# DLRM tower on one core: tiles written out, and masks made from ids in 7 gapped rows of 37

## The reference, cut to what matters

```python
e = jnp.stack([tbl_0[ids[:, 0]], ..., tbl_26[ids[:, 26]]], axis=1)   # [2048, 27, 128], fp32
interactions = jnp.einsum('bfd,bgd->bfg', e, e).reshape(B, 27 * 27)
z = jnp.concatenate([bottom_mlp_out, interactions[:, TRIL_IDX]], axis=1)   # 128 + 351 columns
h = jnp.concatenate([z, bottom_mlp_out], axis=1)                           # 607 columns
h = jnp.maximum(h @ W_top1 + b_top1, 0.0)    # 512
h = jnp.maximum(h @ W_top2 + b_top2, 0.0)    # 256
y = h @ W_top3                               # [2048, 1]
```

## Time and profile before

| | us |
|---|---|
| median of 3 runs | 727.62 |
| lowest and highest | 723.96, 727.86 |
| span of the profiled execution, first to last instruction | 506.4 |
| median less that span | 221.2 |

### The profile page before, as it was taken

One profiled execution on the slowest core, in us unless ns is written; L12 is line 12 of the kernel. 1 busy time (PEld: TensorE's weight loads), 2 busy tenths in 40 slices (PEclk: granted clock), 3 DMA queues, 4 the chain that ended last, 5 costly groups with the idle time before them and its releaser, 6 DMA issues.

```text
span 506.4 us, 7367 instructions
## 1 busy us (share of the span) xinstructions
PE 388.1 (77%) x2708; PEld 353.3 (70%) x2708; DVE 260.2 (51%) x641; ACT 165.4 (33%) x263; POOL 345.1 (68%) x324
## 2 busy tenths in 40 slices
PE   0440878899899589996899589987999689985726
PEld 0440767888788578885788478876888678875516
DVE  0754654945593429742693439551884359330310
ACT  1312252234414323243404433343314341340421
POOL 5877377877787778777877778777877778750000
PEclk9975897999999989997999889997999799997967
DMA  6467212232223221422142221422142222220000
GB/s 154 154 188 218 86 46 64 56 123 63 65 71 107 64 68 45 128 62 62 41 131 63 63 55 46 129 60 70 39 135 62 67 52 52 54 59 10 0 15 1
DMA packets 24792, 38.34 MB, mean 76 GB/s; under 512 B 9436, under 2 KB 17125, under 8 KB 24776
## 3 DMA queue, kind: packets, MB, share of 16 engines
q0 software_dynamic: 10240, 20.99, 15.9%
q1 hardware_dynamic: 14536, 17.12, 11.6%
HBM read 35.00 MB, written 0.01 MB: 69 GB/s over the span
## 4 chain that ended last, share of the span: by engine, by line
POOL 47%; issue 16%; PE 16%; DMA 9%; DVE 6%; ACT 3%; SPq 3%; POOLq 0%; DVEq 0%
POOL rows L203 47%; DMA pairs<-in_tbl 5%; PE gram_bank L531 4%; PE mlp_bank L545 4%; DVE mask L422 3%; PE mlp_bank L556 3%; PE col_bank L506 3%; SPq L229 2%; DMA rowid<-in_row_of_chunk 2%; PE col_bank L492 2%; DVE pairs L455 2%; ACT pairs L334 1%; DMA rows<-in_tbl,idx 1%; ACT eT L322 1%; DMA x<-pairs 1%
## 5 line engine op out<-in xcount | busy, mean ns | idle before, releaser
L203 POOL DMA_INDIRECT rows<-in_tbl,idx x320 | 344.9, 1078 | 106.6 <-issue 96.6
L492 PE MATMUL col_bank<-mask,parts 125*128 125x256 f32 x896 | 121.4, 295 | 46.1 <-DVE mask L422 44.4
L492 PEld LDWEIGHTS col_bank<-mask,parts 125*128 125x128 f32 x896 | 115.0, 201 | 53.7 <-issue 45.1
L531 PE MATMUL gram_bank<-eT 128*122 128x104 f32 x1024 | 119.1, 274 | 19.4 <-DVE pairs L455 8.1
L531 PEld LDWEIGHTS gram_bank<-eT 128*122 128x122 f32 x1024 | 114.8, 189 | 24.9 <-issue 13.3
L422 DVE TENSOR_SCALAR mask<-hot_f,rowid 125x256 fp32r<-125x256 f16 x448 | 131.4, 362 | 0.1
L446 DVE COPY eT<-col_bank 128x512 f32<-128x512 f32 x56 | 59.2, 1057 | 110.6 <-PE col_bank L506 108.7
L322 ACT ACTIVATE eT<-col_bank 128x512 f32<-128x512 f32 (+1 forms) x56 | 55.2, 986 | 168.7 <-PE col_bank L492 101.1
L455 DVE COPY pairs<-gram_bank 26x208 f32<-26x208 f32 x128 | 65.2, 510 | 86.1 <-PE gram_bank L531 84.8
L334 ACT ACTIVATE pairs<-gram_bank 26x208 f32<-26x208 f32 x128 | 67.1, 524 | 85.0 <-PE gram_bank L531 83.9
L545 PE MATMUL mlp_bank<-x,w 126*128 126x256 f32 (+5 forms) x288 | 64.2, 379 | 15.8 <-DMA x<-pairs 15.8
(11 more groups left out here) (10 smaller groups left out, 10.6 us busy)
## 6 DMA issues: line engine op xcount, KB each, us to landing
hot_i<-in_hot_ids SPq DMA_DIRECT2D x8, 896.0 KB
rows<-in_tbl,idx POOLq DMA_INDIRECT x320
pairs<-in_tbl SPq DMA_DIRECT2D x7, 500.0 KB
x<-in_bottom SPq DMA_DIRECT2D x8, 128.0 KB, 2.5
x<-pairs SPq DMA_DIRECT2D x16, 39.0 KB
x<-pairs SPq DMA_DIRECT2D x16, 34.5 KB
w<-in_w SPq DMA_DIRECT2D x1, 512.0 KB
w<-in_w_pairs SPq DMA_DIRECT2D x2, 252.0 KB
```

Of the source, the lines that this page charges most:

```text
L203: pool.indirect_dma_start(out=rows[:, h, n * D:(n + 1) * D], out_offset=None, in_=tables[f], in_offset=bass.IndirectOffsetOnAxis(ap=idx[:, ...
L492: last = nc.tensor.matmul(col_bank[b][:, i * TILE:(i + 1) * TILE], parts[0:ROWS, k, part, c * D:(c + 1) * D], mask[0:ROWS, k % MASKS, c, : ...
L531: last = nc.tensor.matmul(gram_bank[s % 2][0:GRAM_ROWS, q, 0:PACK * (F - 1)], eT[:, a:a + PACK, :].rearrange("p s f -> p (s f)")[:, 0:GRAM ...
```

## The change

All hardware loops are replaced by Python loops, so that every tile is written out. The ids of a table are stored as 7 rows of 37 with one unused element behind each row (a pitch of 38), in `hot_i` and `hot_f`. A mask instruction reads the 7 x 37 ids and writes one run of 259 elements; the matmul takes the first 256. The number of mask instructions, their place in DVE's order and all waits stay. The id DMA and ACT's conversion go over 266 instead of 256 elements a table.

```diff
+ID_ROWS, ID_WIDE = 7, 37
+ID_PITCH = ID_WIDE + 1
+MASK_WIDE = ID_ROWS * ID_WIDE
+MASK_PITCH = MASK_WIDE + 1
+assert MASK_WIDE >= TILE and ID_ROWS % 2 == 1 and MASK_WIDE % 2 == 1
...
-        mask = sb("mask", [128, MASKS, CHUNKS, TILE], f32r)
-        hot_i = sb("hot_i", [128, ONE_HOT, TILE], i32)
-        hot_f = sb("hot_f", [128, ONE_HOT, TILE], fp16)
+        mask = sb("mask", [128, MASKS, CHUNKS, MASK_PITCH], f32r)
+        hot_i = sb("hot_i", [128, ONE_HOT, ID_ROWS * ID_PITCH], i32)
+        hot_f = sb("hot_f", [128, ONE_HOT, ID_ROWS * ID_PITCH], fp16)
...
-            with pool.Fori(0, TILES // 2) as u:
+            for u in range(TILES // 2):
...
-            with sp.Fori(0, (TILES - 4) // 2) as u:
+            for u in range((TILES - 4) // 2):
...
-            with act.Fori(2, TILES - 1) as t:
+            for t in range(2, TILES - 1):
...
+                ids = hot_f[0:ROWS, k, :].rearrange("p (r i) -> p r i", r=ID_ROWS)[:, :, 0:ID_WIDE]
                 for c in chunks:
-                    last = nc.vector.tensor_scalar(mask[0:ROWS, k % MASKS, c, :], hot_f[0:ROWS, k, :],
+                    last = nc.vector.tensor_scalar(mask[0:ROWS, k % MASKS, c, 0:MASK_WIDE], ids,
                                                    rowid[0:ROWS, c:c + 1], None, ALU.is_equal)
...
-            with dve.Fori(1, TILES - 1) as t:
+            for t in range(1, TILES - 1):
...
-                                    mask[0:ROWS, k % MASKS, c, :], start=(c == 0 and part == 0),
+                                    mask[0:ROWS, k % MASKS, c, 0:TILE], start=(c == 0 and part == 0),
...
-            with pe.Fori(2, TILES - 1) as t:
+            for t in range(2, TILES - 1):
```

More of the change, by code:

```diff
@@ L214, in load_hot_ids @@
             def load_hot_ids(t):
-                src = hot_ids_d[bass.ds(t, 1)].rearrange("a k s -> a (k s)").broadcast_to([128, ONE_HOT * TILE])
+                src = hot_ids_d[bass.ds(t, 1)].rearrange("a k s -> a (k s)").broadcast_to([128, ONE_HOT * ID_ROWS * ID_PITCH])
                 sp.dma_start(hot_i[:, :, :].rearrange("p k s -> p (k s)"), src).then_inc(hot_ids_loaded, 16)
@@ L638 @@
     tables = [put(f"in_tbl_{f}", inputs[f"tbl_{f}"]) for f in range(F)]
+    hot_ids = ids[:, ONE_HOT_TABLES].reshape(TILES, TILE, ONE_HOT).transpose(0, 2, 1)
+    hot_ids = np.pad(hot_ids, ((0, 0), (0, 0), (0, MASK_WIDE - TILE))).reshape(TILES, ONE_HOT, ID_ROWS, ID_WIDE)
+    hot_ids = np.pad(hot_ids, ((0, 0), (0, 0), (0, 0), (0, ID_PITCH - ID_WIDE))).reshape(TILES, ONE_HOT, -1)
     args = [
         put("in_gather_ids", ids[:, GATHERED_TABLES].reshape(B // HALF, HALF, GATHERED)),
-        put("in_hot_ids", ids[:, ONE_HOT_TABLES].reshape(TILES, TILE, ONE_HOT).transpose(0, 2, 1)),
+        put("in_hot_ids", hot_ids),
         put("in_bottom", np.asarray(inputs["r_bottom_mlp_out"]).T),
```

## The result

| | before | changed |
|---|---|---|
| median of 4 runs, us | 727.74 | 755.69 |
| lowest and highest | 723.96, 728.01 | 754.26, 765.53 |
| span of the profiled execution | 506.4 | 752.5 |

The ratio is 1.052 [1.039, 1.066]: the changed kernel is slower. The prediction said 718.7 us, with 710.5 to 731.5 as its range, and was wrong. A ratio with a 95% interval behind it goes by the fastest runs of both kernels, any other by their medians.

A forecast was written before the change was run, and what follows sets the result against it. POOL, held up by masks, was the bound; PE and DVE would become the pace. Span 388.6 + 107.4 + 3.12 - 1.58 = 497.5, 8.9 under 506.4, so 727.6 - 8.9 = 718.7 us, range 710.5 to 731.5.

The forecast's parts named there:

- I take the 221.2 us between span and median as fixed: Outside the profiled span: time assumed unchanged, so the span's saving of 8.9 us comes straight off 727.6.
- POOL, with 43 us of blocked gathers: Mid-kernel: POOL sets the pace and loses 43 us because masks hold the shared port against its gather DMAs.
- the prediction's 0.36: look_up masks: start-to-start time taken for the new mask, 0.36 us, between bounds of 0.337 and 0.398.
- The low bound: New masks: pitch 0.337 us, from 0.270 stream plus the 0.067 seen behind a subtraction of 512 elements.
- the slope of 3.3 us: Whole kernel: 332 masks on the path, so each 0.01 us of pitch is 3.3 us; no gain at 0.387.
- the estimate of 0.345: New masks: alternative pitch from the skill's 75 ns behind the stream; the sum would be 14 us faster.
- The mode ends: Masks: odd, unequal counts 7 and 259 end two-at-a-time streaming; 259 elements then stream in 0.270 us.
- Blocked gathers go: POOL's gathers: none over 1.1 us beside masks; a tile of gathers takes 49.9 us without blocking.
- The masks behind the pair copies are all on the path: look_up: 44 masks a tile count in full, adding 3.12 us and making PE's turn 52.36 us.
- Tiles written out cost nothing: Python loops for hardware loops: priced at nothing, bounded by a gain of 3 us and a loss of 5.
- PE's clock stays in look_up: look_up: short idle gaps leave the clock at 1.00; the rival that it falls, +30, 749 us, had 4%.
- That the fixed cost stays in full (16%): Rival on masks: pitch 0.398 or more, +13 us, 731 to 732, slower than before by 4; 16%.

The follow-up runs named there:

- the first set: Slow-level runs: kernel before repeated, new masks with loops kept, tiles written out with old masks; kernel before 730.39 us (712.72 to 740.88).
- the third set: Slow-level runs: changed kernel, its two halves, and old masks with short instructions added; kernel before 717.26 us, changed kernel 760.36.
- The run with short instructions: Kernel before, two of each table's eight masks split into one element and 255; 718.64 us, ratio 1.025 [1.012, 1.037].
- the fourth set: Quick-level runs: changed kernel, gathers of tile 0 alone, plain DMAs, shortened new masks; kernel before 502.91 us, changed kernel 509.24.
- the masks of 185: New masks cut to 5 of 7 rows (185 elements), loops kept; 484.01 us, 0.973 of the kernel before, repeated at 484.18.
- the slow chip's run with 40 gathers: Kernel before with gathers for tile 0 only, 40 instead of 320, rows reused by later tiles, slow level; 477.50 us.
- the quick run with 40 gathers: Kernel before with gathers for tile 0 only, 40 instead of 320, rows reused by later tiles, quick level; 467.00 us, 0.937.

## Why the prediction was wrong

**The step that failed: "I take the 221.2 us between span and median as fixed".** The trace had 506.4 us and the runs 727.6, and the prediction put the difference outside the span. At the slow level the span itself is 725.8 us, and in every run whose span is on record only some 1.8 us lie outside it. The bottleneck read from the first trace (POOL, with 43 us of blocked gathers) doesn't exist there: POOL is busy 308.4 us and waits 149.8 for PE. Two windows of one turn, from gather to gather, before and after (start:end, us, busy PE, PEld, DVE, ACT, POOL, the clock granted, the share and GB/s of the DMA engines):

```profile
318.70:403.70 85.00, 55.41 (x334) 47.73 (x333) 30.66 (x80) 19.30 (x33) 38.11 (x41) 0.78 0.17 48
```

```profile
328.90:417.40 88.50, 57.71 (x334) 48.63 (x333) 36.73 (x80) 19.30 (x33) 37.80 (x40) 0.79 0.17 47
```

A turn is 3.5 us longer here, 88.5 against 85.0 to 85.4 in the steady ones. In the kernel before the timeline has the same turn as this:

```profile
371.88 6.24 DVE L422 TENSOR_SCALAR mask<-hot_f,rowid 125x256 fp32r<-125x256 f16 x20
...
383.27 13.51 PE L492 MATMUL col_bank<-mask,parts 125*128 125x256 f32 x93 [1.03 <-issue]
...
387.85 6.35 DVE L422 TENSOR_SCALAR mask<-hot_f,rowid 125x256 fp32r<-125x256 f16 x24
```

The 20 masks in front are covered by the stall in both. The 24 behind it took 6.35 us and take 9.41: 3.06 a tile, in seven tiles 21.4. Tile 0's 24 masks, 7.29 in the earlier trace rows, take 9.41: 2.1 more. That is 23.5 of the 26.7 us between the two spans (752.5 - 725.8), and of the 27.95 between the medians. The two spans are of different sets, and in the first set the kernel before spreads over 28 us, so that the sum comes so near is partly luck.

At this level a blocked gather even helps. In the third set's trace of written-out tiles with the old masks, two gathers took 5.7 us beside the 20 masks. One of them, with the turn it lies in and a turn without:

```profile
380.19 5.66 POOL L203 DMA_INDIRECT rows<-in_tbl,idx  x1 [0.30 <-issue]
380.43 5.30 DVE L422 TENSOR_SCALAR mask<-hot_f,rowid 125x256 fp32r<-125x256 f16 x20
...
383.45 11.52 PE L492 MATMUL col_bank<-mask,parts 125*128 125x256 f32 x77 [0.34 <-issue]
```

```profile
329.40:408.70 79.30, 55.94 (x334) 49.34 (x333) 31.02 (x80) 19.28 (x33) 42.71 (x41) 0.81 0.19 52
...
489.60:574.50 84.90, 54.58 (x334) 48.29 (x333) 30.76 (x80) 19.27 (x33) 37.95 (x40) 0.78 0.18 49
```

While the gather is blocked no other is issued, and PE works without gaps from 383.45, with gathers of this half still to come. The turn takes 79.3 us instead of 84.9. The run with short instructions has four such gathers (5.33 to 5.90 us), with turns of 79.1, 80.6, 81.8 and 81.8 us against 84.8 without, and the shortest span of all full kernels traced at this level, 710.2. The new masks block no gather and give this up. In the third set the changed kernel lost 43 us, 15 more than in the first; such turns of the kernel before, some 3 to 6 us each, can be a part of it. They aren't shown to be, for its only trace at this level has no gather blocked for 5 us. Some turns of the loop version with new masks took 93 to 96 us instead of 88.5; the cause isn't known.

By the sum of the masks' time, 23.5 us above, no gain was to be had at this level at any pitch above 0.265 us. Even with the prediction's 0.36 it is 7 x 24 x 0.095 + 1.35 = +17 us.

**The second error, a size: the mask's pitch.** The prediction took 0.36 and measured is 0.390. Of that 0.270 is the stream of 259 elements and 0.120 the fixed part, near the steady run's 0.128 and far from the subtraction's 0.067. The low bound, from another operation, was no guide; the same operation's steady run was. With the slope of 3.3 us each 0.01 this costs 10 us, and turns -8.9 into +1.1: at the quick level alone, the forecast would have been no change. Its span, 507.5, meets the measured 506.5 partly by luck: in the fourth set the spans of the kernel before run from 489.6 to 506.4, so the first trace lies at their top, and by the medians the change costs 6.3 us. The Trainium skill's figure behind the estimate of 0.345 (Vector Engine (DVE) Microarchitecture Reference, 5.2: about 75 ns behind the stream) is too low by 45 ns here; the 14 us that the prediction works out with it are against the kernel before.

**Against the prediction's other steps:**
- *The mode ends.* Right: 1.05 ns an element, by the masks of 185. The condition of the Trainium skill (VectorE: DVE Perf Modes, What auto-detection actually checks) held for odd and unequal counts, the case that its other page (Vector Engine (DVE) Microarchitecture Reference, 5.1) has as not measured.
- *Blocked gathers go.* Right: no gather takes over 2 us in any trace with the new masks (at most 1.92 us, 1.995 in the quick run). POOL's busy time fell from 345.1 to 305.3 at the quick level. At the slow one there was little to free: the kernel before has 308.4 there. Beside masks all were to be under 1.1; a few of 1.2 to 1.5 are a small miss.
- *The masks behind the pair copies are all on the path.* Right at the quick level (43.2 us for 332 masks, turn 53.5 to 53.9), wrong at the slow one, where 20 of 44 hide in the stall.
- *Tiles written out cost nothing.* Neither shown nor refuted: 0.993 and 1.019 by the medians, and -7 to -8 us on top of the masks. The instruction queue moved 0.34 instead of 0.18 MB, still 0.2 to 0.3% of the engines' time.
- *PE's clock stays in look_up.* Right at the quick level: 1.00 in the turn from 223.2 to 276.7, in spite of gaps of 1 to 2 us behind each table. At the slow level it is 0.78 and 0.79, but alike before and after.

```profile
223.20:276.70 53.50, 45.20 (x334) 40.93 (x333) 36.80 (x80) 19.35 (x33) 37.73 (x40) 1.00 0.29 78
```

- *The rivals.* That the fixed cost stays in full (16%) was near in its mechanism (0.390, over the 0.387 at which nothing is gained), though its price, 731 to 732, was again a sum on the wrong level. No rival had a kernel in which PE is never held by POOL, so that freeing POOL gives nothing.

## What to carry to other kernels

When a trace's span and the timed median lie far apart, settle first whether both are of the same state of the chip. If that can't be settled, work the change out for both, with the second bottleneck taken as a rival of its own. Wherever a run's span is on record here, it is some 1.8 us under the time, and 221 us outside the span was no sign of overhead but of another state. An edit that frees an engine pays only where this engine is waited for, and can cost where its work disturbs another. Read a fixed cost of an instruction from a steady run of that same operation rather than from a cheaper neighbour.

## What the runs showed of the hardware

- The same program, alone on a core, took about 500 us in three cases (506.4, 499.27, 502.91) and 717 to 751 on others. Within a set of runs the level never changed, except between the first trace and its timed runs.
- At the slow level indirect gathers in flight hold up TensorE: single matmuls start at multiples of about 0.7 us from each other, up to 2.8 apart (3.5 in the slow chip's run with 40 gathers), and copies of its products start up to 20 us after these end. It sets in some 10 us after a half's first gather and ends about 3 us after its last. Plain DMAs from the same queue do nothing of the kind (2.0 instead of 113.1 us of idle). A gather that masks hold back for 5 us lets TensorE go on meanwhile. What differs between the chips, and what part of an indirect gather does it, stays open.
- The chain of waits of the quick run with 40 gathers shows how such a kernel looks without stalls; "issue" is 5% of it:

```profile
PE 66%; DMA 9%; ACT 9%; DVE 7%; issue 5%; SPq 3%; DVEq 0%; ACTq 0%
```

- One-element instructions between two-element ones, two in ten, didn't end the blocking of a gather (5.90 us).
